# A hybrid attention and local-attention kernel: norms through logarithm and exponential, feed-forward by features, token shift by DMA, rotated banks, unrolled steps

## The reference

```python
x = x + attn(layernorm(x)) + stack(layernorm(x))
for i in range(6):                                   # stack
    x = attn_layer(shift_tokens(x), Wqkv[i], q_scale[i], k_scale[i], Wo[i]) + x
    x = ffn_layer(shift_tokens(x), ln_g[i], ln_b[i], W1[i], b1[i], W2[i], b2[i]) + x
```

## Time and profile before

| | us |
|---|---|
| median of 3 runs (lowest, highest) | 1760.35 (1759.22, 1760.85) |
| the profiled execution | 1758.46 |
| its span, first to last instruction | 1756.7 |
| busy in the span: PE, DVE, POOL, ACT | 1647.6, 1623.9, 1550.9, 1325.7 |
| mean granted TensorE clock | 0.985 of full |

### The profile page before, as it was taken

The page is one execution under the profiler, slowest core; times in us unless marked ns, Lnnn a source line. Parts: engine busy times, 40 slices in busy tenths (PEclk is TensorE's granted clock), DMA queues, the critical chain, the costliest instruction groups (busy, mean ns, idle before and its releaser), DMA issues.

```text
span 1756.7 us, 71028 instructions
## 1 busy us (share of the span) xinstructions
PE 1647.6 (94%) x26032; PEld 1357.0 (77%) x26032; DVE 1623.9 (92%) x3652; ACT 1325.7 (75%) x2594; POOL 1550.9 (88%) x1078
## 2 busy tenths in 40 slices
PE   5789999999999999999999999999999999999995
PEld 4568878788887788888778888878888877888773
DVE  6699999999999999999999999999999999999982
ACT  3467787878778787877877778787787878787772
POOL 3398999899999899999989999989999989999970
PEclk9799999999999999999999999999999999999997
DMA  5010011001201101300110310011211001101100
GB/s 149 37 44 24 21 30 33 21 26 31 94 21 30 33 21 30 98 24 21 30 33 21 98 33 21 21 30 33 89 30 33 21 21 30 33 21 30 33 24 25
DMA packets 29948, 65.57 MB, mean 37 GB/s; under 512 B 4949, under 2 KB 16217, under 8 KB 29145
## 3 DMA queue, kind: packets, MB, share of 16 engines
q1 hardware_dynamic: 29912, 65.09, 12.9%
HBM read 19.99 MB, written 1.05 MB: 12 GB/s over the span
## 4 chain that ended last, share of the span: by engine, by line
PE 66%; DVE 18%; issue 9%; ACT 4%; DVEq 1%; POOL 1%; SPq 0%; DMA 0%; ACTq 0%; POOLq 0%
PE bank L1021 51%; PE bank L1146 8%; PE bank L1181 5%; DVE n L834 4%; DVE t L832 2%; DVE es L863 2%; DVE rot L850 2%; PE bank L1223 2%; ACT pz L597 2%; ACT sq L561 2%; DVE t L831 2%; DVE w_lo L806 1%; DVE t L829 1%; DVE n2c L843 1%; PE bank L1096 1%
## 5 line engine op out<-in xcount | busy, mean ns | idle before, releaser
L404 POOL TENSOR_TENSOR rnorm<-n2c,minus_half 128x16 f32<-128x16 f32 x192 | 584.9, 3047 | 6.2 <-DVE n2c L843 0.3
L394 POOL TENSOR_TENSOR rot<-t 128x512 f32<-128x512 f32 x384 | 514.7, 1356 | 68.9 <-DVE t L832 68.9
L1021 PE MATMUL bank<-w_hi,x_hi 128*128 128x512 f32 x576 | 283.0, 491 | 13.1 <-DVE t L832 9.3
L829 DVE TENSOR_TENSOR t<-bank,rtab 128x512 f32<-128x512 f32 x384 | 260.6, 679 | 36.3 <-ACT sq L561 30.8
L417 POOL TENSOR_TENSOR es<-es,r 128x512 f32<-128x512 f32 x192 | 221.3, 1152 | 76.7 <-DVE r L873 76.7
L597 ACT ACTIVATE pz<-bank 64x512 f32<-64x512 f32 x384 | 226.3, 589 | 52.2 <-PE bank L1181 47.4
L1146 PE MATMUL bank<-ident,rot 128*128 128x128 f32 x1536 | 238.6, 278 | 28.8 <-DVE rot L850 17.5
L834 DVE TENSOR_REDUCE n<-sq 128x8 f32<-128x512 f32 x384 | 259.3, 675 | 0.0
L561 ACT ACTIVATE sq<-bank 128x512 f32<-128x512 f32 x384 | 224.6, 596 | 17.0 <-PE bank L1021 13.5
L1146 PEld LDWEIGHTS bank<-ident,rot 128*128 128x128 f32 x1536 | 182.4, 142 | 70.2 <-DVE rot L850 28.5
L1021 PE MATMUL bank<-w_hi,x_lo 128*128 128x512 f32 x576 | 229.7, 399 | 0.0
(11 more groups left out here) (101 smaller groups left out, 3340.6 us busy)
## 6 DMA issues: line engine op xcount, KB each, us to landing
vb<-v SPq DMA_DIRECT2D x96, 384.0 KB, 3.4
w_new<-in_Wqkv SPq DMA_DIRECT2D x6, 1536.0 KB, 8.4
vb<-v SPq DMA_DIRECT2D x48, 128.0 KB, 2.3
w_o<-in_Wo SPq DMA_DIRECT2D x6, 512.0 KB
w<-in_W SPq DMA_DIRECT2D x6, 341.0 KB
b<-in_b SPq DMA_DIRECT2D x6, 341.0 KB
out<-acc SPq DMA_DIRECT2D x1, 1024.0 KB, 5.1
w<-in_W SPq DMA_DIRECT2D x12, 64.0 KB
```

The source lines that it names most:

```text
L394: g.tensor_tensor(rot[:, i * CH:(i + 1) * CH], t1[:, b:b + CH], t2[:, b:b + CH], ALU.add)\
L404: g.tensor_tensor(rnorm[:, w], n2c[:, w], minus_half[:, :], ALU.pow).then_inc(s_rn, 1)
L829: d.tensor_tensor(heads(t1[:, b:b + CH]), src, table(n, kind, T), ALU.mult).then_inc(s_t1, 1)
L1021: return t.matmul(o, l, r, start=start, stop=stop, skip_group_check=True)
```

## The change

The change rewrites the order of a step on every engine and much of what a step consists of.

- **Norms.** The power on POOL goes. ACT does four small instructions on 128 x 32 for each tile (`guard`, `logarithm`, `first_root`, `half_square`), DVE two for a Newton step (`newton_half`, `newton_root`). One function table, chosen by number (`exp_and_log`), serves exponential and logarithm.
- **Rotation.** The two half products become one of 512 columns with the halves read in reversed order. POOL scales all eight chunks; DVE none. POOL takes over `split_lo` and `normalise`.
- **Feed-forward by features.** `hidden(n, j)` makes features on partitions and 256 tokens on columns, for three chunks j, so that bias enters gelu and the product with the gate is the input of `down` as it is. `turn_h`, `take_h`, `bias_gate` and `bias_hidden` go. All of it lives in one bank, `pF`.
- **Token shift by DMA.** SP moves the tokens for the projection (`load_x`) and for the feed-forward (`load_xs`) with four DMAs each. `turn_mid`, `turn_shifted`, `shifted_f`, `copy_in` and `residual` go.
- **Banks.** Twelve products rotate over three banks instead of two for q and k and three shared ones for v.
- **Loops** are unrolled, and a step spreads over five iterations (n to n - 4). b1 is loaded by features, six DMAs of 4-byte elements behind the first weights, and these count in `s_const` (19 loads).
- In the dense attention ACT also splits the first weights, one chunk after each of the first six sequences.

```diff
-            def norms(n, T, k):
-                w = slice((2 * T + k) * HEADS, (2 * T + k + 1) * HEADS)
-                pool.wait_ge(s_n2c, nth(4, n, 2 * T + k + 1))
...
-                g.tensor_tensor(rnorm[:, w], n2c[:, w], minus_half[:, :], ALU.pow).then_inc(s_rn, 1)
+            def logarithm(n, T):
+                act.wait_ge(s_n2c, nth(TILES, n, T + 1))
+                a.activation(logs[:, norms(T)], n2c[:, norms(T)], ACT.Ln, bias=tiny[:, 1:2]).then_inc(s_log, 1)
+            def first_root(n, T):
...
+                a.activation(root[:, norms(T)], logs[:, norms(T)], ACT.Exp, scale=-0.5).then_inc(s_root, 1)
...
+            def newton_root(n, T):
...
+                d.scalar_tensor_tensor(out=rnorm[:, norms(T)], in0=newton[:, norms(T)], scalar=1.5,
+                                       in1=root[:, norms(T)], op0=ALU.subtract, op1=ALU.mult).then_inc(s_rn, 1)
...
+            def hidden(n, j):
+                pe.wait_ge(s_xg, n + 1)
+                for half in range(2):
+                    w = (par(n) * 2 + half) * HID + j * P
+                    last = mm(pF[0:width(j), half * LEN:(half + 1) * LEN], w_1[:, w:w + width(j)], xg[:, :])
+                last.then_inc(s_hid, 1)
...
+            def gelu(n, j):
+                act.wait_ge(s_hid, nth(HCH, n, j + 1))
+                act.wait_ge(s_hm, nth(HCH, n - 1, j + 1))
...
+                if j == HCH - 1:
+                    exp_and_log()
...
+            def shifted(n, dst, signal):
...
+                sp.dma_start(dst[16:P, :, h:], src[15:P - 1, :, h:]).then_inc(signal, 16)
+                sp.dma_start(dst[1:16, :, h:], src[0:15, :, h:]).then_inc(signal, 16)
+                sp.dma_start(dst[0:1, 1, h:], src[P - 1:P, 0, h:]).then_inc(signal, 16)
+                sp.dma_start(dst[:, :, 0:h], src[:, :, 0:h]).then_inc(signal, 16)
...
+            def iteration(n):
+                if live(n - 4):
+                    later_weights(n - 4)
+                if live(n - 2):
+                    copy_v1(n - 2)
+                if live(n):
+                    load_x(n)
+                if live(n - 3):
+                    load_xs(n - 3)
+                if live(n - 2):
+                    copy_v0(n - 2)
```

More of the change, by code:

```diff
@@ new lines, in copy_v1, with later_weights @@
+            def copy_v1(n):
+                for c in range(4):
+                    sp.wait_ge(s_v[c], n + 1)
+                sp.wait_ge(s_av, nth(4, n - 1, 4))
+                sp.dma_start(vb[0:WIN, INNER:], v[P - WIN:P, 0:INNER]).then_inc(s_vb[1], 16)
+                sp.dma_start(vb[WIN:P, INNER:], v[0:P - WIN, INNER:]).then_inc(s_vb[1], 16)
+            def later_weights(n):
+                if n % SEQS == 0 and 0 < n // SEQS < DEPTH - 1:
+                    l = n // SEQS + 1
+                    sp.wait_ge(s_xready, n)
+                    weights(l)
+                    qkv_weights(l)
@@ L350, in _ @@
+            sp.wait_ge(s_zero, 2)
+            def iteration(n):
[9 more added lines that the diff above has]
+                    copy_v0(n - 2)
+            for n in range(STEPS + DEEP):
+                iteration(n)
             sp.wait_ge(s_fin, 1)
@@ new lines, in next_hi, with exp_and_log @@
+            def next_hi(n, c):
+                if n % SEQS == SEQS - 1 and n < STEPS - 1:
+                    split_hi(layer(n) + 1, c)
+            for s in range(-1, SEQS + 1):
+                first_attention(s)
+                if 0 <= s < WCH:
+                    split_hi(0, s)
+            def exp_and_log():
+                a.add_instruction(mybir.InstLoadActFuncSet(name=nc.get_next_instruction_name(),
+                                                           engine=mybir.EngineType.Activation, act_func_set_id=6))
@@ L703, in _ @@
-            split_hi(0, (0, 1))
-            for n in range(-2, FIRST):
-                iteration(n)
-            with act.Fori(FIRST, LAST) as n:
-                iteration(n)
-            for n in range(LAST, STEPS + 2):
+                act.wait_ge(s_xnt, n + 1)
+                act.wait_ge(s_hid, nth(HCH, n - 1, HCH))
+                l = layer(n)
+                a.activation(xg[:, :], pF[:, 0:LEN], ACT.Identity, bias=shift[:, l:l + 1], scale=gain[:, l:l + 1])\
+                 .then_inc(s_xg, 1)
@@ L1005, in _, with gated @@
-            split_lo(0, (0, 1))
-            for n in range(-2, FIRST):
-                iteration(n)
-            with dve.Fori(FIRST, LAST) as n:
-                iteration(n)
-            for n in range(LAST, STEPS + 2):
-                iteration(n)
-            dve.wait_ge(s_xready, STEPS + SEQS)
+            def gated(n, j):
+                dve.wait_ge(s_gg, nth(HCH, n, j + 1))
+                dve.wait_ge(s_down, n)
+                w, o, c = width(j), j * DEPTH + layer(n), slice(j * LEN, (j + 1) * LEN)
+                d.scalar_tensor_tensor(out=ht[0:w, c], in0=pF[0:w, 0:LEN], scalar=b_1[0:w, o:o + 1], in1=gt[0:w, c],
+                                       op0=ALU.add, op1=ALU.mult).then_inc(s_hm, 1)
@@ L1084, in _ @@
                 first_attention(s)
[L1085 to L1087 removed]
+            for s in range(2, SEQS + 1):
                 first_attention(s)
@@ L1354, in _ @@
-            for n in range(-2, FIRST):
-                iteration(n)
-            with pe.Fori(FIRST, LAST) as n:
-                iteration(n)
-            for n in range(LAST, STEPS + 2):
+                        k = width(j) + (j == HCH - 1)
+                        c, w = j * LEN + T * P, (par(n) * HCH + j) * P
+                        last = mm(pF[:, T * P:(T + 1) * P], ht[0:k, c:c + P], w_2[0:k, w:w + P],
+                                  start=j == 0, stop=j == HCH - 1)
+                last.then_inc(s_down, 1)
```

1173 lines of the change are left out of this document (561 added, 612 removed).

## The result

The changed kernel takes 1828.2 us (median of 4 runs, 1822.73 to 1831.91) against 1760.0 us before: 1.0385 times as long (95% interval 1.036 to 1.041). It is slower by 68 us, where 1706 us had been forecast. The profiled execution took 1831.9 us, its span is 1830.1.

The account below looks back on a forecast made before the run. PE's work plus about 0.7 us of waits a step was taken as the bound; 1758.46 - 57.6 (steps) - 8.7 (borders) + 11.8 (start) = 1704, given as 1706 us for the median, range 1686 to 1748.

Parts of the forecast that it names:

- PE's work, engines' loads: A step: PE 32.3 us without waits, from 33.7; DVE 25, POOL 25, ACT near 26, none of them the bound.
- The one tight path: From product of v's fourth chunk to project(n, 0), through ACT, SP, DVE: 16.3 us against 16.2 of PE work, no slack.
- The issues: SP's ten DMA issues on the path to copy_v0's landing: 0.57 us each, 5.7 us; at most 0.7 each allowed.
- nothing in this trace is under 0.4: Lower bound on the price of a DMA issue, in us, read from the earlier trace; its rows had 0.53 to 0.59.
- Where PE would wait: If the path is late, PE idles ahead of `w_hi,x_hi`, released by `x_lo`, every step.
- The sum of the steps: 48 steps at 32.5 us instead of 33.7, with 0.2 us of waits each: -57.6 us.
- the DMA queue decides: Rival, chance 0.11: kernel slower; at 0.8 us per DMA issue PE waits 2.3 us a step, 1807 us.
- The border: Layer borders: splitting new weights moves from full DVE to POOL, extra 3.74 us falls to 2, five times: -8.7 us.
- The start: Before the steps: b1's loads +8.4 us, ACT's weight splits +2.4, first step -3, filling and draining +4: +11.8 us.
- The table loads: Two ACT table switches on the path; the skill's drain would add 2.8 us, about 1835 us; left out of the sum.
- Unrolling: Writing out the loops neither gains nor costs, from iteration 46's 33.67 us: priced at zero.

Follow-up runs that it names:

- e10: Changed kernel with SyncE's order copy_v0, shift of xin, copy_v1, shift of xs, and b1's loads behind the first two layers' weights with their own semaphore: 1651.2 us.
- e13: Kernel before, looped, without the first of the two swapped products of rotate (output not the reference's): 1735.6 us, ratio 0.986.
- e14: Kernel before without the first of the two swapped products, with all loops written out: 1730.2 us, ratio 0.982.
- e7: Changed kernel with SyncE's order copy_v0, shift of xs, shift of xin, copy_v1, and b1's loads behind the first two layers' weights with their own semaphore: 1907.8 us.

## Why the prediction was wrong

- **PE's work, engines' loads.** Right. 32.3 us a step were forecast as the floor; e10 shows 32.05. The `hidden` blocks start 0.87 us apart (0.94 forecast), a swapped product with reversed halves takes 0.68 us, a scaling on POOL 1.04. DVE, ACT and POOL are busy 26.1, 26.0 and 25.6 us (25, 26 and 25). `normalise` was undersized: 0.80 us for one, not at most 0.6; it has no effect.
- **"The one tight path" is the step that failed.** The path was the right one, with all its stations; its length was wrong. From the end of the product of v's fourth chunk to `project(n,0)` pass 18.9 us (1531.22 to 1550.10), of which PE works 16.0 (16.2 forecast) and idles 1.77 + 1.09. The path was forecast at 16.3. *The issues* are the mis-sized term: ten for 5.7 us at 0.57, "since size has no visible effect on the issue", and 7.36 measured here, 7.85 on average. The DMAs of a shift cost 0.64, 0.94, 0.59 and 0.66 by their medians, and 0.04 to 0.12 stand between two. The mean of 0.74 lies above the 0.70 that I allowed at most: two DMAs of another shape gave no bound. That is +1.7 us in this step and +2.1 on average. *ACT* needs 4.3 us to the copied v, not 3.7, because `pz` and an exponential stand ahead: +0.6. The hand-overs and the last piece add 0.3.
- **A reading that was wrong.** That "nothing in this trace is under 0.4" does not hold, and the rows taken were too narrow at the top as well. SyncE's queue in the kernel before has these, both of shapes other than v's copies, and they show that an issue's price varies with what is moved:

```profile
11.32 3.08 SPq L304 DMA_DIRECT2D w<-in_W  x1
...
17.04 0.24 SPq L309 DMA_DIRECT2D w<-in_b  x1
```

- **Where PE would wait.** I expected it ahead of `project(n,0)` alone. The landing holds the values block first, and behind it 3.6 us of ACT and DVE stand against 2.5 us of values and scores on PE, which gives the second wait.
- **The sum of the steps.** They average 35.55 us instead of 32.7 (border shares included): 47 x 2.85 = 134 us. The step of 35.02 shown above makes 109 of them. The program's pieces on SyncE's queue make some 20 more, an estimate. What is left falls to the borders and the low clock, which was not in the sum at all.
- **The rival "the DMA queue decides"** (0.11) is what happened, at 0.74 us an issue in the step shown and 0.78 on average, against its 0.8. Its 1807 us were 21 low; ACT's 0.6 us and the 0.3 of the hand-overs are not in it. With a path computed as 16.3 against 16.2, eight of whose ten issues were of a shape not in the trace, it deserved more than 0.11, and the range should have held it.
- **The border** (-8.7): right in sign; in e10 no layer's border costs over 1.7 us. **The start** (+11.8): PE's first transposes at 24.86 us, 6.1 later than before, against 8.4 forecast; ACT's splits cost nothing, one sequence of the dense attention takes 4.0 us as before, since they fill ACT's waits. Outside the steps the kernel was 6 us better than the sum (1831.9 less 47 x 35.55 is 161; 1704 less 47 x 32.7 is 167).
- **The table loads.** In the earlier trace rows no drain showed; in the changed kernel gelu starts 1.30 us behind the start of its load again. The Trainium skill's 1380 ns of drain (ScalarE: Activation LUTs, What ACT_TABLE_LOAD costs) is not borne out here, and its 1835 us came near the result by another cause.
- **Unrolling** (0): wrong for the kernel before, where it costs 27 us: one step outside the loop did not show what 44 in a row do. Near zero by e13 and e14, where DVE has room. Wrong again for the changed kernel by some 20 us, the estimate above.

## What to carry to other kernels

An in-order DMA queue is an engine like the others: lay its issues into the step's timeline with their own durations, place each by when its wait ends as well as by when its data is needed, and put what many wait for ahead of what few do. Here the same eleven issues in six orders gave 1651 and 1703 us (with b1 apart), 1691, 1716, 1828 and 1915. Where a path equals its cover to 0.1 us and rests on a price that the trace lacks, forecast both sides of it.

## What the runs showed of the hardware

- An issue on SyncE costs 0.55 to 0.94 us by shape, 0.93 for 15 partitions against 0.64 for 112; behind a DMA of 127 partitions the next issue takes 2.7 to 4.0 us. Six strided loads of b1 take 8.55 us of queue (1.4 each; 4.7 us forecast for the six), and 5.42 in e7, behind the weights.
- A 16 KB load of instructions beside an issue on SyncE often lengthens it. In the changed kernel, between 110 and 1600 us, 25 of 48 issues with such a load during them or up to 0.7 us ahead take over 0.2 us more than the median of their line, and 1 of 406 others does.
- PE's granted clock falls to 0.50 for some 3 us behind idle pieces of 1.8 to 3.6 us, 21 times in the steps of the changed kernel, and stays at 1.00 behind others of up to 3.24.
- Writing out a kernel's loops changed its time by +1.5% with DVE 96% busy and by -0.3% with 3.3 us of room in a step.
